# Layer norms of an eight-layer transformer: the epsilon added by VectorE in place of GpSimd, and layer 0's weight splits at another place of GpSimd's queue

## What is computed

```python
x = x + 0.5 * ffn(layernorm(x), w_up, w_down)      # ternary weights, 128 -> 512 -> 128
x = x + attn(layernorm(x), ...)                    # eight layers, below
x = x + 0.5 * ffn(layernorm(x), w_up, w_down)

def _ln(x, scale, bias):
    m = jnp.mean(x, axis=-1, keepdims=True)
    v = jnp.var(x, axis=-1, keepdims=True)
    return (x - m) * jax.lax.rsqrt(v + EPS_LN) * scale + bias

for i in range(8):
    residual = x
    Q = elu(x @ Wq[i] + bq[i]) + 1.0
    K = elu(x @ Wk[i] + bk[i]) + 1.0
    value = x @ Wv[i] + bv[i]
    KV = jnp.einsum('nsh,nsh->nh', K, value)
    Ksum = jnp.sum(K, axis=1)
    V = Q * KV[:, None, :] / (Q * Ksum[:, None, :] + EPS_ATTN)
    x = _ln(gelu(V @ Wo[i] + bo[i]) + residual, ln1_s[i], ln1_b[i])
    residual = x
    x = _ln(gelu(gelu(x @ W1[i] + b1[i]) @ W2[i] + b2[i]) + residual, ln2_s[i], ln2_b[i])
```

## Time and profile before

| | us |
|---|---|
| median of 3 runs | 934.0 |
| lowest, highest | 932.17, 934.82 |
| the profiled execution's own time | 936.12 |
| its span in the profile | 934.3 |
| busy in the span: TensorE | 865.6 (93%) |
| VectorE | 813.2 (87%) |
| ScalarE | 795.5 (85%) |
| GpSimd | 441.9 (47%) |
| mean granted clock of TensorE | 0.956 of full speed |

### The profile page before, as it was taken

The page is one execution under the profiler, slowest core; times in us unless marked ns, Lnnn a source line. Parts: engine busy times, 40 slices in busy tenths (PEclk is TensorE's granted clock), DMA queues, the critical chain, the costliest instruction groups (busy, mean ns, idle before and its releaser), DMA issues.

```text
span 934.3 us, 14522 instructions
## 1 busy us (share of the span) xinstructions
PE 865.6 (93%) x4043; PEld 613.2 (66%) x4043; DVE 813.2 (87%) x3333; ACT 795.5 (85%) x1138; POOL 441.9 (47%) x561
## 2 busy tenths in 40 slices
PE   3999358999999999999999999999999999995898
PEld 2899235666666666666666666666666666653797
DVE  6477456999999999999999999999999999967553
ACT  3685477999999999999999999999999999742873
POOL 3242702455555555455555555555555445433221
PEclk8799678999999999999999999999999999995999
DMA  5000100000000000000000000000000000000011
GB/s 151 1 1 1 33 1 1 9 1 15 20 1 15 1 21 1 14 13 9 1 15 12 9 4 12 20 1 15 1 12 1 1 1 0 1 1 0 13 34 46
DMA packets 19518, 12.05 MB, mean 13 GB/s; under 512 B 1160, under 2 KB 18288, under 8 KB 19440
## 3 DMA queue, kind: packets, MB, share of 16 engines
q1 hardware_dynamic: 19440, 11.13, 4.1%
HBM read 9.03 MB, written 2.10 MB: 12 GB/s over the span
## 4 chain that ended last, share of the span: by engine, by line
DVE 64%; PE 19%; issue 7%; ACT 6%; POOL 2%; DMA 0%; SPq 0%; DVEq 0%; ACTq 0%; POOLq 0%
DVE z L859 16%; DVE st L845 10%; PE bank L542 6%; DVE phi_k L982 5%; DVE x_fm L1069 5%; DVE kvf L993 4%; DVE phi_q L972 4%; DVE mv L852 4%; DVE e L965 4%; DVE vf L1034 3%; PE bank L556 3%; DVE x_hi L1077 3%; PE bank L392 3%; DVE y L1042 2%; PE bank L529 2%
## 5 line engine op out<-in xcount | busy, mean ns | idle before, releaser
L1300 POOL TENSOR_TENSOR x_lo<-x_fm,x_hi 128x512 fp32r<-128x512 f32 x120 | 155.5, 1305 | 261.0 <-DVE x_hi L1077 261.0
L493 PE MATMUL bank<-h,w 128*128 128x512 f32 x512 | 260.5, 593 | 0.0
L737 ACT ACTIVATE h<-bank,par 128x512 f32<-128x512 f32 x256 | 167.1, 693 | 11.7 <-PE bank L400 10.6
L859 DVE TENSOR_SCALAR z<-bank,mv,rstd 128x128 f32<-128x128 f32 x512 | 169.4, 403 | 8.4 <-POOL rstd L1292 8.2
L398 PE MATMUL bank<-x_hi,w_hi 128*128 128x512 f32 x256 | 151.6, 592 | 1.6 <-ACT h L737 1.6
L1292 POOL TENSOR_TENSOR rstd<-ve,minus_half 128x4 f32<-128x4 f32 x128 | 132.7, 1037 | 10.7
L398 PE MATMUL bank<-x_hi,wqkv_hi 128*128 128x512 f32 x192 | 107.6, 560 | 17.0 <-DVE phi_q L972 10.0
L845 DVE BATCH_NORM_STATS2 st<-bank 128x6 f32<-128x128 f32 x512 | 113.3, 285 | 1.0 <-PE bank L392 0.9
L392 PEld LDWEIGHTS bank<-ident,y 128*128 128x128 f32 x512 | 62.4, 141 | 59.9 <-ACT x_fm L753 23.4
L400 PE MATMUL bank<-x_hi,w_lo 128*128 128x512 f32 x256 | 101.1, 395 | 0.0
L399 PE MATMUL bank<-x_lo,w_hi 128*128 128x512 f32 x256 | 100.9, 394 | 0.0
(11 more groups left out here) (101 smaller groups left out, 1797.3 us busy)
## 6 DMA issues: line engine op xcount, KB each, us to landing
x_tm<-in_x SPq DMA_DIRECT2D x8, 256.0 KB, 3.8
raw_w<-in_W SPq DMA_DIRECT2D x8, 256.0 KB, 2.7
w<-in_W SPq DMA_DIRECT2D x8, 256.0 KB, 2.8
out<-x_tm SPq DMA_DIRECT2D x8, 256.0 KB, 2.3
raw_qkv<-in_Wk SPq DMA_DIRECT2D x8, 64.0 KB, 1.8
raw_qkv<-in_Wq SPq DMA_DIRECT2D x8, 64.0 KB, 2.0
raw_qkv<-in_Wv SPq DMA_DIRECT2D x8, 64.0 KB, 1.9
wo<-in_Wo SPq DMA_DIRECT2D x8, 64.0 KB, 2.5
```

What stands on the lines that cost most here:

```text
L493: mm = pe.matmul(m.ps_o[:, :], m.w2[T.weights][:, c, :], m.h[:, T.par, c, :], start=c == 0, stop=c == FC - 1)
L737: act.activation(m.h[:, T.par, c, :], m.ps_h[c % 2][:, :], ACT.Gelu_apprx_tanh, bias=column(m, B1, T.layer, c, FC)).then_inc(s.gelu_h[T.pa ...
L859: last = dve.tensor_scalar(dst[:, j, :], src(j), mv[:, j, 0:1], scale[:, j:j + 1], ALU.subtract, ALU.mult)
L1300: pool.tensor_tensor(m.x_lo[:, T.slot, :], m.x_fm[:, T.slot, :], m.x_hi[:, T.slot, :].bitcast(F32), ALU.subtract).then_inc(done, 1)
```

## The change

```diff
-TICK_QKV, TICK_W1 = -19, -1
+TICK_QKV, TICK_W1 = -29, -29
...
     def means(T, i):
...
         block_means(dve, m.st[i][:, T.par], m.mv[i][:, T.par], (s.stats1, s.stats2)[i], T.n, (s.mv1, s.mv2)[i])
+        dve.wait_ge((s.mv1, s.mv2)[i], T.n)
+        at_least(dve, (s.rstd1, s.rstd2)[i], T.n - 2)
+        dve.tensor_scalar(m.ve[i][:, T.par, :], m.mv[i][:, T.par, :, 1], EPS_LN, None, ALU.add).then_inc((s.ve1, s.ve2)[i], 1)
...
 def gpsimd_tick(pool, m, s, f, tick):
...
-    def var_eps(T, i):
-        if not T:
-            return
-        pool.wait_ge((s.mv1, s.mv2)[i], T.n)
-        pool.tensor_scalar(m.ve[i][:, T.par, :], m.mv[i][:, T.par, :, 1], EPS_LN, None, ALU.add).then_inc((s.ve1, s.ve2)[i], 1)
...
-    var_eps(l(0, 1), 0)
...
-    var_eps(l(0, 2), 1)
...
-    var_eps(l(1, 1), 0)
...
-    var_eps(l(1, 2), 1)
```

## The result

| | before | after |
|---|---|---|
| median, us (4 runs each) | 933.1 | 951.9 |
| lowest, highest | 932.1, 934.8 | 949.7, 954.3 |
| the profiled execution's own time | 936.12 | 954.26 |
| its span | 934.3 | 952.5 |

The ratio is 1.020 (95% interval 1.017 to 1.023): 18.8 us slower, where the prediction had 14.2 us and a range that ends at 955.

A forecast was written before the change was run, and what follows sets the result against it. VectorE was taken to bound the dense stage. Additions +21.7, handover -6.1, drain -1.2 and first layer -0.2 us sum to +14.2, on the median of 934.0 a forecast of 948 us, range 941 to 955.

The forecast's parts named there:

- What bounds the kernel: Dense stage, 180 to 805 us: VectorE waits for nobody, so added work lengthens the round; relieving GpSimd there buys nothing.
- Together 0.19 us: Each addition moved to VectorE: 0.11 us wait on its own engine plus 0.08 us step; 114 in the dense stage, +21.7 us.
- The wait costs, a free one does not explain it: Own-engine wait behind VectorE's aggregates costs 0.11 us; the rival, a free wait, gives 935.6 us, chance 0.05.
- The second semaphore at nothing: The addition's other wait, for rstd of two tiles earlier, was raised long before and is priced at nothing.
- The handover, -6.1: First feed-forward part to layers: earlier splits let the first projection start about 104.0 instead of 110.13 us, 6.1 us off.
- Cost: nothing: The six splits fit GpSimd's 6.36 us idle hole before 73.00 us, ending near 71.3, so moving them costs nothing.
- The drain, -1.2: Layers' end after 805 us: rstd comes earlier for z, 0.3 us for three single tiles, 0.9 for three pairs; 0.4 to 2.
- The additions meet GpSimd: Rival: in each dense round a fourth addition waits up to 0.6 us for a GpSimd power; 965 us, chance 0.06.
- TensorE down to about 97%: Sign of being right: TensorE's busy share between 180 and 805 us falls to about 97% as the round lengthens.

The follow-up runs named there:

- e4: e1 with VectorE waiting for its own aggregates behind each group, additions still on GpSimd; 945.2 us, ratio 1.012, 17.4 us slower than e1.
- e5: e1 plus a spare, non-waiting addition on VectorE behind each group of aggregates, real additions still on GpSimd; 936.2 us, ratio 1.001, 8.4 us slower than e1.
- e6: e1 without the layers' epsilon additions, GpSimd taking the power of the bare variance, so epsilon is missing from the result; 926.9 us, ratio 0.992.
- e1: The kernel before with only the six layer-0 weight splits moved up, additions still on GpSimd; 927.8 us, ratio 0.993, 6.7 us faster.
- e3: The changed kernel with each VectorE addition one step later, behind the work that followed its aggregates; 939.1 us, ratio 1.004.
- e7: e1 with GpSimd waiting for the eighth tile's normalisation (z_c) before its first x_lo; 928.6 us, ratio 0.993.

## Why the prediction was right, and where it was off

- **What bounds the kernel**: right. Both a wait and an instruction put on VectorE lengthened the round (e4 and e5, separately), and GpSimd with 128 operations less bought nothing in the dense stage (e6).
- **"Together 0.19 us"** for an addition: 0.22 measured (0.219), and this term is most of the miss, 114 x 0.029 = 3.3 us of the 4.6 between 14.2 and 18.8. Both of its parts held: the wait 0.12 (predicted 0.11), the own step 0.078 (0.08). Left out was the follower, 0.026 us longer once it no longer stands behind the aggregates. The pair in the earlier trace rows could not show it, since it was read only as far as the start of the follower; a pair with and without the addition, read one instruction further, is what was missing. The range of 0.16 to 0.21 was too narrow for the same reason. The other terms add 0.7 in the profiles: the drain gave 0.6 us less than forecast and the first part took 0.8 more, while the handover gave 0.2 more and the last part was 0.5 shorter. With the 3.3 that is the 4.0 between 14.2 and the spans' 18.2; the 0.6 between spans and medians lies within the interval.
- **The wait costs, a free one does not explain it**: right; e4 alone has 17.4 us of it. The Trainium skill, VectorE: DVE Perf Modes, section The DRAIN you can't avoid, says that a semaphore costs nothing extra, since the next operation waits for the pipeline anyway; it adds that an operation which isn't held starts earlier. This case's measurement decides against the free semaphore behind such small instructions: an independent follower starts 0.08 us before the end of the aggregates' record, one that waits on them 0.03 to 0.04 us behind it (398.56 + 0.38 to 398.98 in e4).
- **The second semaphore at nothing**: nothing speaks against it; the wait measured with mv's semaphore alone (e4) and the instruction (e5) already make up the whole price.
- **The handover, -6.1**: -6.3 measured, for the reason named. The first projection is now held only by its turn behind the eighth tile's transposes.
- **"Cost: nothing" for the splits in the first part**: nearly. The six end at 72.67 us and not at 71.3: one cast took four times its length (1.0 us more), and this execution is 0.4 us later already in front of them. On GpSimd, in the hole of the earlier trace rows:

```profile
67.00 0.29 POOL L1260 CAST wqkv_hi<-raw_qkv 128x128 fp32r<-128x128 f32 x1
...
69.31 1.29 POOL L1260 CAST w_hi<-raw_w 128x128 fp32r<-128x128 f32 x1
...
72.22 0.45 POOL L1262 TENSOR_TENSOR w_lo<-raw_w,w_hi 128x128 fp32r<-128x128 f32 x1
73.81 1.01 POOL L1316 TENSOR_TENSOR scale<-scale,plus_half 128x4 f32<-128x4 f32 x1 [1.14 <-DVE scale L1101]
```

  The hole is still 1.14 us deep at its end, yet the stage became 0.35 us longer: from the power in front of the hole to the one behind it 7.79 us in e1 (64.86 to 72.65), 7.36 before (65.64 to 73.00), and of these 0.4 some 0.35 are still there at the last power. The cast ran beside VectorE's sum of squares (69.16 to 70.45). VectorE was held too: in e1 against before the sum took 1.30 us for 1.23, the addition behind it 0.25 for 0.16 and four fz_c a little later 1.36 for 1.11, 0.4 us together. The rest of the +0.8 up to the last power, 0.4 us, is there already at the power in front of the hole (66.04 us, and 65.64 before), ahead of everything that the change moved, so it belongs to the spread of this part between executions (last section).
- **The drain, -1.2**: -0.6, half of it, though within the 0.4 to 2 allowed. A single tile:

```profile
850.40 0.17 DVE L1059 TENSOR_SCALAR ve<-mv 128x4 f32<-128x4 f32 x1
851.69 1.36 DVE L859 TENSOR_SCALAR z<-bank,mv,rstd 128x128 f32<-128x128 f32 x4 [1.12 <-POOL rstd L1289]
```

  z's wait fell from 1.47 to 1.12, but 0.21 of that is VectorE's own addition; from mv's end to z it is 0.14 us less, near the 0.1 of the prediction. The idle column alone would say 0.35. Not all of this reaches the end: from this z to the next tile's it takes 6.38 us (851.69 to 858.07), and 6.39 before (832.92 to 839.31). In the pairs the shorter z came as forecast, 2.64 us for 2.80. Why the whole drain gives only half of the sum was not traced further.
- **The additions meet GpSimd**: did not happen in that form. All 128 take 169 to 173 ns. The powers are what got longer, a mean of 1174 ns where they were 1037:

```profile
L1059 DVE TENSOR_SCALAR ve<-mv x128: 169/170/173, 133.8 to 862.3; 128x4 f32<-128x4 f32 x128
L1289 POOL TENSOR_TENSOR rstd<-ve,minus_half x128: 1000/1008/1381, 134.0 to 862.6; 128x4 f32<-128x4 f32 x128
```

  A power now starts just behind its addition. From 200 to 780 us the 51 that start beside an e take 1.37 to 1.38 us and the other 51 take 1.00 to 1.01; nobody waits for them in the rounds.
- **"TensorE down to about 97%"**: wrong. It shows 645.49 of 650 us, 99.3%, with the same matmuls in a round 4% longer. Its records grew with the round: of 200 to 780 us it is busy for 580.00 in 2503 matmuls before and for 576.96 in 2400 after, 0.232 and 0.240 us for each. So a full row of TensorE doesn't show that it has no slack.

## What to carry to other kernels

On an engine that sets the round, price an instruction by the change of the distance between its neighbours on both sides, with and without it, and read to the start of the second instruction behind it. An instruction that reads what its own engine has just written costs mostly the wait, not its work: the same additions one instruction further down cost less than half (e3), and on an engine with idle time they cost nothing in the rounds (e6 against e1). Two edits in one change are best timed apart; here the good one, 6.7 us, was buried under the other's 24.

## What the runs showed of the hardware

- VectorE: a 128x4 addition whose record is 0.15 to 0.17 us long costs 0.071 us when independent, and 0.219 when it reads the aggregates directly before it. The wait without any instruction costs 0.151: a start 0.12 us later, and 0.033 more in the step of the instruction that waited.
- A follower holds VectorE 0.026 us less when it stands directly behind these aggregates with no wait in between (seen with e, 0.576 for 0.602, and phi_q, 0.635 for 0.661).
- VectorE and GpSimd hold each other up in certain pairs, in both directions: the first part's normalisation (fz_c) 4.88 us beside x_lo and 1.12 without, e 1.85 for 0.69 beside x_lo, a cast on GpSimd 1.29 for 0.29 beside the sum of squares, a power 1.38 for 1.01 beside e. Only the first pair was taken apart (e7); the others coincide in time wherever they are seen. The 128x4 additions and the power did not disturb each other. The Trainium skill, SBUF — State Buffer, section Who interferes with whom, has an exclusive lock between the two for the whole instruction; the first four pairs agree with it. The long small power does not: nine pieces of fz_c before, and ten in the changed kernel, started while a power ran, and took their usual 0.33 to 0.35 us, where each took 1.2 to 1.3 beside x_lo.
- The first part takes different times in different executions, and its longest go with a lower granted clock near its end. From 88 to 92 us in the profile of the kernel before and then in e1:

```profile
88.00:92.00 4.00, 4.00 (x24) 4.00 (x24) 2.10 (x11) 1.00 (x2) 1.96 (x2) 0.61 0.00 0
```

```profile
88.00:92.00 4.00, 3.24 (x30) 3.00 (x28) 3.21 (x17) 1.88 (x4) 1.64 (x2) 1.00 0.01 2
```

  24 matmuls at 0.61 (part of the stretch at the lower of the two levels, 1.2 GHz) against 30 at 1.00. In the 4 us before, the clock was 0.96 and 1.00, and TensorE was busy for 3.74 us in both. The changed kernel and e3 have 0.57 from 88 to 92 us. In these three profiles the last power of the first part starts at 96.97 to 97.75 us, in the six others at 93.37 to 95.39. The profiled executions of before and e1 lie 8.5 us apart where the medians have 6.7, and 2.0 of the 8.5 are there at that power (96.97 and 94.93) already. What sets the clock lower in some executions stays open.
